# Layer norms on GpSimd: subtract mean times rstd instead of adding a product with the negated mean

## What is computed

```python
def _layernorm(x, axis=-1, eps=1e-05):
    m = jnp.mean(x, axis=axis, keepdims=True)
    v = jnp.var(x, axis=axis, keepdims=True)
    return (x - m) / jnp.sqrt(v + eps)

x = x + xattn(_layernorm(x), ctx, ctx, mask, ...)   # one head of 16, its output tiled 16 times, then Wo
x = x + ffn(_layernorm(x), w1, b1, w2, b2)          # 256 -> 1024 -> 256, signs of w times alpha, gelu
```

## Time and profile before

| | |
|---|---|
| median of 3 runs | 383.99 us (382.73 to 384.77) |
| the profiled execution | 381.3 us, its span 379.5 us |
| PE busy | 309.1 us (81%) |
| DVE busy | 286.4 us (75%) |
| ACT busy | 261.4 us (69%) |
| POOL busy | 237.6 us (63%) |
| mean granted TensorE clock | 0.919 of 2.4 GHz |

### The profile page before, as it was taken

One profiled execution on the slowest core, in us unless ns is written; L12 is line 12 of the kernel. 1 busy time (PEld: TensorE's weight loads), 2 busy tenths in 40 slices (PEclk: granted clock), 3 DMA queues, 4 the chain that ended last, 5 costly groups with the idle time before them and its releaser, 6 DMA issues.

```text
span 379.5 us, 6245 instructions
## 1 busy us (share of the span) xinstructions
PE 309.1 (81%) x2087; PEld 206.6 (54%) x2087; DVE 286.4 (75%) x637; ACT 261.4 (69%) x334; POOL 237.6 (63%) x412
## 2 busy tenths in 40 slices
PE   5867714466989898979898989897979799999994
PEld 3533612323656565657565656565656565766664
DVE  1782357378798989897898889885989798886554
ACT  1155532057979796959796969794879788896780
POOL 1213023748659795967688868896588865847521
PEclk9975675568999999989999999998999999999999
DMA  8920022535637674756566756675375736331402
GB/s 260 383 98 3 0 56 61 119 103 111 173 66 200 104 213 68 205 97 191 87 182 111 205 87 177 115 194 100 92 187 134 171 93 139 89 71 56 113 0 111
DMA packets 83263, 47.67 MB, mean 126 GB/s; under 512 B 73496, under 2 KB 76704, under 8 KB 83232
## 3 DMA queue, kind: packets, MB, share of 16 engines
q1 hardware_dynamic: 82320, 47.24, 50.3%
q10 hardware_dynamic: 912, 0.05, 0.2%
HBM read 21.19 MB, written 8.39 MB: 78 GB/s over the span
## 4 chain that ended last, share of the span: by engine, by line
PE 36%; DVE 25%; DMA 22%; issue 9%; ACT 3%; SPq 2%; POOL 1%; DVEq 0%; POOLq 0%
PE psZ L1352 13%; DMA xT_hi<-ctxT 12%; PE psY L1337 9%; DMA x_in<-in_x 9%; DVE x L817 5%; DVE h_lo L826 4%; PE psW L1295 3%; DVE w_sb L733 3%; DVE w_sb L840 3%; DVE st_raw L703 3%; PE psW L1210 2%; PE psW L1316 2%; ACT V_hl L583 1%; SPq L296 1%; SPq L302 1%
## 5 line engine op out<-in xcount | busy, mean ns | idle before, releaser
L1352 PE MATMUL psZ<-sgn2T,h_hi 128*128 128x256 f16 x512 | 117.1, 276 | 0.0
L1352 PE MATMUL psZ<-sgn2T,h_lo 128*128 128x256 f16 x512 | 116.9, 275 | 0.0
L569 ACT ACTIVATE psY<-psY,b_col,alpha1x 128x512 f32<-128x512 f32 x128 | 93.2, 748 | 27.7 <-PE psY L1337 25.6
L1337 PE MATMUL psY<-xT_hi,sgn1T 128*128 128x512 f16 x256 | 99.0, 387 | 8.3 <-DVE h_lo L826 8.1
L1337 PE MATMUL psY<-xT_lo,sgn1T 128*128 128x512 f16 x256 | 98.5, 385 | 0.0
L826 DVE SCALAR_TENSOR_TENSOR h_lo<-psY,h_scale,h_hi 128x1024 f16<-128x1024 f32 x64 | 81.0, 1266 | 16.1 <-ACT h_hi L578 16.0
L481 POOL TENSOR_TENSOR w_sb<-w_sb,x1b 128x256 f32<-128x256 f32 x62 | 43.1, 727 | 57.3 <-DVE w_sb L840 57.3
L578 ACT ACTIVATE h_hi<-psY,h_scale 128x1024 f16<-128x1024 f32 x64 | 71.3, 1114 | 5.9 <-ACT psY L569 0.4
L1352 PEld LDWEIGHTS psZ<-sgn2T,h_hi 128*128 128x128 f16 x512 | 50.6, 99 | 10.8 <-issue 1.9
L1352 PEld LDWEIGHTS psZ<-sgn2T,h_lo 128*128 128x128 f16 x512 | 50.7, 99 | 9.2
L470 POOL TENSOR_TENSOR x1b<-x,b_bc 128x256 f32<-128x256 f32 x64 | 54.3, 881 | 0.3
(11 more groups left out here) (150 smaller groups left out, 439.8 us busy)
## 6 DMA issues: line engine op xcount, KB each, us to landing
x_in<-in_x SPq DMA_DIRECT2D x16, 512.0 KB, 5.6
ctx_sb<-in_x SPq DMA_DIRECT2D x16, 512.0 KB, 4.4
out_x<-w_sb SPq DMA_DIRECT2D x15, 512.0 KB, 3.0
w_sb<-in_L_ffn_w SPq DMA_DIRECT2D x2, 1024.0 KB, 9.1
ctx_sb<-in_ctx SPq DMA_DIRECT2D x1, 1024.0 KB, 6.8
out_x<-w_sb SPq DMA_DIRECT2D x2, 256.0 KB, 2.1
wk_sb<-in_L_xattn_Wk SPq DMA_DIRECT2D x1, 256.0 KB, 3.3
wq_sb<-in_L_xattn_Wq SPq DMA_DIRECT2D x1, 256.0 KB, 3.6
```

Of the source, the lines that this page charges most:

```text
L569: nc.scalar.activation(y, y, ACT.Gelu, bias=b1_col[:, c:c + 1], scale=alpha1x[:, c:c + 1]).then_inc(gelu_done, 1)
L1337: last = nc.tensor.matmul(psY[q % 2][:, c % 2, :], sgn1T[:, k, c * P:(c + 1) * P], part[b % 2][:, :, k, :], start=(n == 0), stop=(n == 2 * ...
L1352: last = nc.tensor.matmul(Z[n][:, (j % 2) * D:(j % 2 + 1) * D], part[q][:, u, j * P:(j + 1) * P], sgn2T[:, 2 * q + u, :], start=(q == 0 an ...
```

## The change

It drops `nmean` and its instruction. `nmr` becomes `mr` = mean times rstd, read straight from the statistics, and the four instructions of L446 multiply and then subtract instead of multiplying and adding. With one instruction fewer each norm raises `norm_steps` by 3 instead of 4, and the wait ahead of the power is for the step of `vare` alone.

```diff
-        nmean = [sb(f"nmean{n}", [P, T]) for n in range(2)]
         vare = [sb(f"vare{n}", [P, T]) for n in range(2)]
         rstd = [sb(f"rstd{n}", [P, T]) for n in range(2)]
-        nmr = [sb(f"nmr{n}", [P, T]) for n in range(2)]
+        mr = [sb(f"mr{n}", [P, T]) for n in range(2)]
...
                 nc.gpsimd.tensor_scalar(vare[n][:, :], st[n][b % 2][:, :, 1], 1.0, EPS, ALU.mult, ALU.add) \
                     .then_inc(norm_steps[n], 1)
-                nc.gpsimd.tensor_scalar(nmean[n][:, :], st[n][b % 2][:, :, 0], -1.0, 1.0, ALU.mult,
-                                        ALU.mult).then_inc(norm_steps[n], 1)
-                pool.wait_ge(norm_steps[n], val(b, 4, 2))
+                pool.wait_ge(norm_steps[n], val(b, 3, 1))
                 nc.gpsimd.tensor_tensor(rstd[n][:, :], vare[n][:, :], mhalf[:, :], ALU.pow) \
                     .then_inc(norm_steps[n], 1)
-                pool.wait_ge(norm_steps[n], val(b, 4, 3))
-                nc.gpsimd.tensor_tensor(nmr[n][:, :], nmean[n][:, :], rstd[n][:, :], ALU.mult) \
+                pool.wait_ge(norm_steps[n], val(b, 3, 2))
+                nc.gpsimd.tensor_tensor(mr[n][:, :], st[n][b % 2][:, :, 0], rstd[n][:, :], ALU.mult) \
                     .then_inc(norm_steps[n], 1)
...
-                pool.wait_ge(norm_steps[n], val(b, 4, 4))
+                pool.wait_ge(norm_steps[n], val(b, 3, 3))
                 for j in range(T):
                     last = nc.gpsimd.tensor_scalar(xh[n][b % 2][:, j, :], src[:, j, :],
-                                                   rstd[n][:, j:j + 1], nmr[n][:, j:j + 1],
-                                                   ALU.mult, ALU.add)
+                                                   rstd[n][:, j:j + 1], mr[n][:, j:j + 1],
+                                                   ALU.mult, ALU.subtract)
                 last.then_inc(normed[n], 1)
```

## The result

The changed kernel takes 418.5 us (414.82 to 420.95, four runs) against 383.82 for the kernel before: a ratio of 1.0897, 95% interval 1.0804 to 1.0989. It is 9% slower, where "no change" was forecast, and outside the range. The profiled execution took 414.8 us with a span of 412.6.

The account below looks back on a forecast made before the run. PE was taken as busiest and the loop as a ring through DVE, with POOL hardly on the path. All parts were worth 0 except the time shift's -0.2 us: 383.99 to 383.8 us, range 381.4 to 386.6.

Parts of the forecast that it names:

- Multiply and subtract instead of multiply and add: L446's tiles on POOL: as fast as now, 0.54 us each, up to 0.8 more; the lower end taken.
- rival (d): Subtracting is slower at L446; POOL absorbs 1.83 us a step without V: +4 to some 35 us, chance 0.05.
- The dropped instruction: Each norm on POOL 0.28 us shorter, 9.0 us over 32 norms, swallowed by idle time ahead of L481: worth 0.
- The shift in time: POOL's xh tiles 0.28 us earlier meet DVE's L783 and L733 differently: -0.7 to +0.5 us, -0.2 taken.
- rival (b): POOL's fourth xh tile gets in ahead of DVE's L733: +0.5 us, 384.5; with the forecast 0.68.
- its test for who comes first: At L733, whichever of DVE's instruction and POOL's tile issues first, even by 0.03 us, holds the port for its whole length.
- L783's place: DVE's L783 gains 0.2 to 0.27 us in three steps, loses 0.15 to 0.23 in others: -0.4 us in sum.
- rival c: PE's clock falls once more or once less in the loop: 381.4 or 386.6 us, chance 0.09 each way.

Follow-up runs that it names:

- The doses: The changed kernel with multiply-subtract in only two or four tiles a step instead of eight: 379.85 us with two, 389.64 and 387.86 with four.
- e6: The changed kernel with multiply-subtract only in norm 1 and multiply-add in norm 0, four slow tiles a step: 387.86 us, ratio 1.0116 to the kernel before.
- e1: The changed kernel with its subtraction turned back into an addition, all else of the change kept: 382.04 us, ratio 0.9942 to the kernel before.
- e8: The changed kernel with multiply-subtract only in the first of a norm's four tiles, multiply-add in the others: 379.85 us, ratio 0.9928 to the kernel before.
- v1: The kernel before with the mean-rstd product dropped, xh as (x plus negated mean) times rstd, add first: 382.62 us, ratio 0.9938.

## Why the prediction was wrong

**The step that failed** is "Multiply and subtract instead of multiply and add". It gave the range from "as fast as now" to the power's extra 0.8 us, and took the lower end, with "the nearest row is L446 itself, same operands, same size". The tile measured 1.21 us: 0.66 above that end, and not far below the other. L446 is nearest in everything but what the change alters, the operation; the row that told something of an odd operation's price was the power's. The argument in rival (d) was worse: that L430 and L432 take 0.20 us each with add and with multiply. At 4 elements a partition the difference of 2.5 ns an element is 0.01 us, which no row would show, and both are pairs of the fast kind anyway. (d) had 0.05 where the rows gave no reason for so little.

**What (d) priced was right in form.** It names the place (L446), the mechanism (store and loads late on SP's queue) and the threshold: 1.83 us a step without V, and 3.63 + 0.27 + 0.56 = 4.46 with V. With the measured 0.66 a tile it gives (5.28 - 1.83) x 5 + (5.28 - 4.46) x 6 = 22 us for eleven steps; 25.5 were measured. That the two are so near is partly luck: the five steps without V grew by 14.4 us where this sum has 17.3, and the six with V by 11.1 where it has 4.9. Once POOL's list fills the step, steps of both kinds last 21.0 to 22.3 us. The remaining 7.6 us of the span lie outside the eleven steps, where (d) had put nothing. Of the 3.4 ahead of them, the first norm's longer tiles are 2.66 - 0.28 = 2.4; the other 1.0 was there before any norm began (DVE's first statistics start at 15.55 instead of 14.56). The 4.2 behind them are ACT's waits for norm 1. The doses bear out that there is a threshold: nothing is left at two tiles. For four it gave 4 us where 4.6 to 6.4 over the kernel before were measured, but in e6 the eleven steps are no longer than before (2.3 us longer than in e1; the fall of the clock told of below is missing in both), and its excess lies ahead of and behind them.

**The dropped instruction** was right in its size (0.28 us a norm, the power at 0.28 after L429) and in that POOL turns it into idle time: e1 has 61.5 us ahead of L478 where the kernel before had 57.3. The kernels with it came out faster than forecast, though: e1, e8 and v1 have ratios of 0.993 to 0.994, some 2 to 3 us, where that part's own bounds were -0.7 to +0.5; the nearer ends of the three intervals lie at -0.7, -1.3 and -0.8 us (v1's medians differ by only 0.6). The next two parts say what that was in e1.

**The shift in time** moved little, and rival (b) can be judged: the tile didn't get in ahead of L733. In four of e1's five steps without V, DVE's L730 is at 1.22 us (1.39 in the fifth); but the held-up tile then runs into the next instruction. Before and e1, the same place of two steps, DVE and then POOL's held-up tile:

```profile
206.37 1.31 DVE L733 SCALAR_TENSOR_TENSOR w_sb<-xh,w_sb 128x1024 f16<-128x1024 f32 x1
207.61 0.43 DVE L765 COPY_PREDICATED sc<-mask_sb,masked_sb 128x256 f32<-128x256 uint8 x1
...
206.59 1.77 POOL L446 TENSOR_SCALAR xh<-x_in,rstd,nmr 128x256 f32<-128x256 f32 x1
```

```profile
205.85 1.22 DVE L730 SCALAR_TENSOR_TENSOR w_sb<-xh,w_sb 128x1024 f16<-128x1024 f32 x1
206.98 0.72 DVE L762 COPY_PREDICATED sc<-mask_sb,masked_sb 128x256 f32<-128x256 uint8 x1
...
205.76 1.64 POOL L443 TENSOR_SCALAR xh<-x_in,rstd,mr 128x256 f32<-128x256 f32 x1
```

Before, the tile waited for the rest of L733 and for L765 as well, and ended 0.33 us behind L765; in e1 it gets in between the two, and L762 waits. So the prediction's reading that L733 alone holds it up was wrong too, and so was its test for who comes first: in e1 the tile starts 0.09 us ahead of L730 (0.07 and 0.08 in two other steps), and it is still the tile that waits. That the two exclude each other, the lengths bear out; that the one which starts first wins, as the prediction used the rule, they do not: the start in the trace does not say who gets through. I had not listed L765 among the instructions that can be held up. L783's place did not change as worked out either: at 201.94 it took 0.62 us and in e1 0.61, while in e8, where the tiles lie differently, it took 0.41, L730 1.22 and L762 0.44, and the step was 17.7 us instead of 18.4. So part of the gain hangs on which DVE instruction meets which tile: it is at most some 0.7 us of the 2.7 by which e1's eleven steps are shorter.

**The clock** (rival c) is the other part of that gain. The other 2.0 us are one step: the one that took 22.07 us with a granted clock of 0.92 in the kernel before takes 20.06 at 1.00 in e1. e8 and e6 have it at 1.00 too (20.10 and 20.31 us), and v1 has the fall again. First e1, then v1, as in the earlier trace rows:

```profile
251.28:271.34 20.06, 17.25 (x127) 11.53 (x125) 17.09 (x38) 15.87 (x20) 14.51 (x24) 1.00 0.60 139
254.39:276.49 22.10, 18.90 (x126) 12.23 (x125) 17.14 (x38) 15.88 (x20) 14.25 (x24) 0.92 0.57 127
```

The other executions agree: of e1's twelve, the three with a mean granted clock of 0.927 or 0.928 took 378.7 to 380.5 us, the six at 0.915 to 0.917 took 381.9 to 383.1. So (c) came true in part in e1, with the sign and about the size that it had; whether the shorter norm makes the fall rarer, or it was chance, no run decides.

In the changed kernel the clock fell more often: 0.892 over the span instead of 0.919, and PE waits longer for its transposes, 42.3 us instead of 29.1. In the eleven steps the falls did not lengthen the step: the three at 0.84 took 21.0 to 21.5 us, the four at 1.00 took 21.7 to 22.3. What they add ahead of these steps and behind them was not separated.

## What to carry to other kernels

On GpSimd, write an affine step as multiply-add, add-multiply or multiply-multiply, with the sign folded into a small operand; the four other pairs tried took 1.22 us for 256 elements a partition instead of 0.55, and multiply-subtract, the one tried at three sizes, cost four times as much per element. Price a changed operation by a row that has that operation, at that size, and where there is none, let the range and the chances say so. An engine with idle time at one point of its ring hides extra work only up to that idle time; beyond it the extra work comes back in every step.

## What the runs showed of the hardware

- A GpSimd instruction with one tensor and two scalars took 0.34 us + 0.83 ns an element for multiply with add, and 0.37 us + 3.3 ns for multiply with subtract; at 128x256 subtract-multiply, add-add and multiply-max took 1.22 as well. The Trainium skill (GPSIMD Engine Reference, "Elementwise — side-by-side cycle accounting") says that a body of at most two operations is bound by its ports at 1.03 cycles an element, with a clock of 1.2 GHz. Multiply-add agrees, 0.83 ns being 1.0 cycle; multiply-subtract, 4.0 cycles, does not, and the measurement decides.
- One operation alone (0.91 us at 128x256) is slower than the two of multiply-add (0.55).
- DVE's COPY_PREDICATED also stretches beside a GpSimd tile, from 0.43 to 0.72 us, as L783 and L733 do. The Trainium skill (SBUF — State Buffer, "Who interferes with whom") states the exclusion for DVE instructions with two SBUF inputs; it agrees, with mask and data both in SBUF.
- L435's 0.20 us became 0.94 to 1.22 in four of 32 norms of the changed kernel, as it then met a DVE instruction that held it up (here L730, which reads two tiles in SBUF and runs from 263.46 to 264.68):

```profile
263.62 1.11 POOL L435 TENSOR_TENSOR mr<-st,rstd 128x4 f32<-128x4 f32 x1
```
